# Moving the fourth group's table gathers on the Pool queue of a DLRM tower kernel, from the first group's period to a place ahead of the second group's pair products

## The reference

```python
e = jnp.stack([tbl_0[ids[:, 0]], ..., tbl_38[ids[:, 38]]], axis=1)      # 512 x 39 x 16
Xi = X0 = e
for W, b in ((W0, b0), (W1, b1), (W2, b2)):                             # 128 outputs each
    Wr = W.reshape(H, F0_, Fi)
    Xi = jnp.einsum('hjk,bjd,bkd->bhd', Wr, X0, Xi) + b[None, :, None]
    res.append(Xi.sum(axis=2))
z = jnp.concatenate(res, axis=1)
h = jnp.concatenate([z, dense_ctx], axis=1)
h = jnp.maximum(h @ W_top1 + b_top1, 0.0)
h = jnp.maximum(h @ W_top2 + b_top2, 0.0)
y = h @ W_top3
```

## Time and profile before

| | |
|---|---|
| median of 3 runs | 651.46 us (650.66 to 651.82) |
| the profiled execution's own time | 650.99 us |
| span of its trace | 649.2 us |
| PE busy | 625.8 us (96% of the span) |
| DVE busy | 563.4 us (87%) |
| ACT busy | 554.7 us (85%) |
| POOL busy | 478.2 us (74%) |
| gathers on POOL (L498) | 160, mean 954 ns |

### The profile page before, as it was taken

One profiled execution on the slowest core, in us unless ns is written; L12 is line 12 of the kernel. 1 busy time (PEld: TensorE's weight loads), 2 busy tenths in 40 slices (PEclk: granted clock), 3 DMA queues, 4 the chain that ended last, 5 costly groups with the idle time before them and its releaser, 6 DMA issues.

```text
span 649.2 us, 11457 instructions
## 1 busy us (share of the span) xinstructions
PE 625.8 (96%) x2630; PEld 478.4 (74%) x2630; DVE 563.4 (87%) x878; ACT 554.7 (85%) x1941; POOL 478.2 (74%) x533
## 2 busy tenths in 40 slices
PE   2899999999999999999999999999999999989998
PEld 2766677787777777777878777777777777767784
DVE  2658878999999999999898989999999999899880
ACT  2558889999999999999999999999999989989772
POOL 7657898888888888888888888888888647062700
PEclk9999999999999999999999999999999999999999
DMA  8264623333333242423424233333332420300000
GB/s 297 26 117 111 127 28 85 54 87 61 88 55 81 59 87 55 81 62 54 92 32 103 35 86 55 87 58 82 59 82 59 88 49 2 95 3 0 2 1 0
DMA packets 91117, 43.58 MB, mean 67 GB/s; under 512 B 80630, under 2 KB 83780, under 8 KB 88943
## 3 DMA queue, kind: packets, MB, share of 16 engines
q1 hardware_dynamic: 84058, 41.77, 29.0%
q0 software_dynamic: 5120, 1.29, 2.2%
q10 hardware_dynamic: 1904, 0.15, 0.2%
HBM read 36.39 MB, written 1.81 MB: 59 GB/s over the span
## 4 chain that ended last, share of the span: by engine, by line
PE 85%; DMA 6%; ACT 3%; POOL 2%; DVE 1%; issue 1%; SPq 1%; ACTq 0%; DVEq 0%; POOLq 0%
PE yb L1126 20%; PE yb L1130 20%; PE yb L1127 20%; PE p L1091 8%; PE pq L1103 5%; DMA late<-x_scratch 4%; DMA gram<-in_L_rec_W_dram 2%; ACT yb L767 1%; POOL late L573 1%; PE yb L1239 1%; PE p L1184 1%; PE p L1086 1%; PE p L1085 1%; PE p L1088 1%; PE p L1216 1%
## 5 line engine op out<-in xcount | busy, mean ns | idle before, releaser
L767 ACT ACTIVATE yb<-yb,x0t 128x128 f32<-128x128 f32 x1728 | 465.1, 391 | 47.7 <-PE yb L1130 44.7
L937 DVE TENSOR_TENSOR acc<-acc,yb 128x512 f32<-128x512 f32 (+1 forms) x512 | 324.3, 671 | 31.6 <-ACT yb L767 29.5
L1126 PE MATMUL yb<-w1h,x1h 128*128 128x512 f32 (+1 forms) x640 | 284.7, 445 | 4.3 <-DVE acc L937 3.3
L1130 PE MATMUL yb<-w1h,x1l 128*128 128x512 f32 (+1 forms) x640 | 247.8, 387 | 0.0
L1127 PE MATMUL yb<-w1l,x1h 128*128 128x512 f32 (+1 forms) x640 | 247.3, 386 | 0.0
L498 POOL DMA_INDIRECT emb<-in_table_dram,idx x160 | 152.6, 954 | 47.7 <-issue 44.3
L1126 PEld LDWEIGHTS yb<-w1h,x1h 128*128 128x128 f32 x640 | 120.1, 188 | 53.1 <-DVE acc L937 16.1
L1127 PEld LDWEIGHTS yb<-w1l,x1h 128*128 128x128 f32 x640 | 120.5, 188 | 34.4 <-issue 11.3
L1130 PEld LDWEIGHTS yb<-w1h,x1l 128*128 128x128 f32 x640 | 120.1, 188 | 24.9 <-DVE x1l L898 0.4
L573 POOL TENSOR_TENSOR late<-late,x0r 117x512 f32<-117x512 f32 (+1 forms) x105 | 132.7, 1295 | 5.0 <-DMA late<-x_scratch 3.9
L916 DVE TENSOR_TENSOR acc<-yb,x0t 128x512 f32<-128x512 f32 x128 | 88.1, 688 | 13.2 <-PE yb L1130 13.2
(11 more groups left out here) (125 smaller groups left out, 416.9 us busy)
## 6 DMA issues: line engine op xcount, KB each, us to landing
late<-x_scratch SPq DMA_DIRECT2D x45, 312.0 KB
late<-x_scratch SPq DMA_DIRECT2D x30, 234.0 KB
x0r<-x_scratch SPq DMA_DIRECT2D x15, 234.0 KB
emb<-in_table_dram,idx POOLq DMA_INDIRECT x160
gram<-in_L_rec_W_dram SPq DMA_DIRECT2D x1, 2496.0 KB, 11.5
late<-x_scratch SPq DMA_DIRECT2D x15, 156.0 KB
spare<-spare SPq DMA_DIRECT2D x28, 78.0 KB
x_scratch<-emb SPq DMA_DIRECT2D x75, 20.0 KB
```

Of the source, the lines that this page charges most:

```text
L767: op = act.activation(part, part, ACT.Copy, scale=x0t[u][:, t, j:j + 1])
L937: dve.tensor_tensor(part, part, parts(y_bank(t, m), n), ALU.add).then_inc(summed, 1)
L1126: pe.matmul(y[:, 0:w], hi, w1h[:, at:at + w], start=True, stop=False)
L1130: pe.matmul(y[:, 0:w], lo, w1h[:, at:at + w], start=False, stop=True).then_inc(bank_ready, 1)
```

## The change

The ten gathers of group 3 (the fourth group), with their two index additions and their two waits, leave period 0 of POOL and stand directly behind the gathers of group 2. `low_weights` moves from ahead of chunks 0 to 3 of group 1 to behind them. Period 0 of POOL holds no gathers any more; all other periods are as before.

```diff
                 if i < CHUNKS:
                     pool.wait_ge(pairs_ready, i + 1)
                 gather(0, i)
+            pool.wait_ge(embq_ready, 2)
+            pool.wait_ge(x0d_out, 16 * STORES)
+            rows_of(3, 1)
+            pool.wait_ge(idx_ready, 2 * 4)
+            for i in range(PER_Q):
+                gather(1, i)
...
             def period(g, u, after):
 
-                todo = list(range(PER_Q)) if after > 2 else []
+                ahead = isinstance(g, int) and g == 0
+                todo = list(range(PER_Q)) if after > 2 and not ahead else []
                 for t in range(TILES):
-                    if t == 0 and after > 2:
+                    if t == 0 and after > 2 and not ahead:
                         pool.wait_ge(embq_ready, g + 2)
                         pool.wait_ge(x0d_out, (g + 1) * (16 * STORES))
                         rows_of(g + 3, 1 - u)
...
-            low_weights()
             for c in range(EARLY):
                 pair_chunk(1, c)
+            low_weights()
             period(0, 0, 3)
```

## The result

| | before | changed |
|---|---|---|
| median of 18 runs of each on the same chip | 651.56 us (650.66 to 652.25) | 653.72 us (651.66 to 655.33) |
| ratio, 95% interval | | 1.0028 [1.0021, 1.0036] |
| profiled execution | 650.99 us | 651.66 us |
| its span | 649.2 us | 649.9 us |

The change makes the kernel slower by more than its measurement leaves open: 2.16 us in the medians, 0.28% in the ratio, which stands for 1.8 us. The forecast was +1.0 us, 652.5, with a top of 653.6. The median lies 0.1 us above that top; by the ratio, on the prediction's 651.46 us, the kernel comes to 653.3, inside the range near its upper end. One execution of the changed kernel took 1625.01 us and is left out of the range and the ratio; no trace shows why.

The account below looks back on a forecast made before the run. PE was taken to bound the kernel from 118 to 560 us, so earlier losses stay. New stall 2.43 us, less old 1.53, plus 0.1 remaining, gives +1.0 on 651.46: 652.5 us, 8-in-10 range 651.5 to 653.6.

Parts of the forecast that it names:

- The new stall: Chunk 0 of group 1: the ten gathers end at 56.08, so PE stands 2.43 us where it had not waited.
- The second stall and the chain: Chunk 0 of group 2: old PE stall 1.53 us; POOL and SP run later, leaving a loss of 0.90 to 1.2 us.
- the late transfer: Group 2's rows: `load_rows` and its transfer come 2.9 us later and land at 80.2 if the transfer gains nothing.
- PE's own arrival: Chunk 0 of group 2: PE gets there at 81.41 if nothing else holds it, a loss of 0.90 us.
- Cover of `bdiag`: Group 1's first tile: `bdiag` ready at 63.1, PE wants it at 63.42; covered by 0.3 us.
- The sum: First two periods: 2.43 us new stall, less 1.53 of the old, plus 0.1 remaining: +1.0 us.
- the likeliest case: Whole kernel: the forecast of +0.7 to +1.3 us, by itself 652.1 to 652.8 us; chance 0.55.
- a chain that overruns: Chunk 0 of group 2: transfer gains nothing and POOL is another 0.1 us or more late; 652.8 to 653.3; chance 0.25.
- gathers that back up: POOL ahead of group 1: gathers wait for earlier ones to land; partial back-up of 1.5 us gives 654.0; chance 0.07.
- The stall was there: Against a rival at chunk 0 of group 1: gathers fill only POOL's idle time, no new stall, 649.9; faster: 0.05.
- PE's clock falls in the longer stall: Behind the 2.43 us stall: matmuls at half speed cost 0.5 us per us; three give 654.0; chance 0.05.
- The signs that the prediction listed for being wrong: In the trace: gathers beyond 1.25 us a step, PE waiting for `bdiag`, or PE losing new time beyond 82 us.

Follow-up runs that it names:

- `e1_again`: The changed kernel run once more with no edit; 653.95 us, ratio 1.0041 to the kernel before.
- `e5_swap_alone`: The kernel before with only `low_weights` moved behind chunks 0 to 3 of group 1, gathers unmoved; 653.33 us, ratio 1.0030.
- `e6_low_first`: The changed kernel with `low_weights` put back ahead of chunks 0 to 3 of group 1, so the gathers' move alone; 655.06 us, ratio 1.0059.
- `e4_split9`: The changed kernel with nine gathers ahead and one behind `sum_dims`; 650.62 us, ratio 0.9993 to the kernel before.
- the filled kernels: The changed kernel with 20 or 10 extra identity transposes on PE ahead of chunk 0 of group 1; 0.93 and 0.83 us slower than before.
- `e2_pe_filled`: The changed kernel with 20 identity transposes on PE ahead of chunk 0 of group 1, into bank `p0`; 0.93 us slower than before.

## Where the prediction held and where it failed: its steps one by one

**The new stall: right.** The gathers ended at 55.98 (56.08 was worked out), chunk 0 on POOL began at 55.99 (56.1), and PE stood 2.38 us (2.43). PE's distance behind the product was 1.44 us, as taken from the second stall.

**The second stall and the chain: right, at the lower bound.** `load_rows` came at 66.64 (66.9), chunk 4 at 62.86 (63.1), and POOL had chunk 0 of group 2 at 79.51, where 80.34 was worked out from the late transfer. Of the two times that meet there PE's own arrival decided, with 81.37 - (79.51 + 1.44) = 0.42 us to spare. That is the lower end, +0.90; the rows give +0.86. The prediction made this hang on the transfer: from SP's issue to POOL's start it took 79.51 - 66.64 = 12.87 us, against 77.28 + 0.14 - 64.01 = 13.41 before, sooner by 0.54 us and so by more than the 0.4 that the prediction asked for. In `e1_again` it took 11.44 us, from 66.39 to 77.83, so it also differs from one execution to the next.

**Cover of `bdiag`: held.** PE's matmul on it runs at 63.38 without a wait.

**The sum: right for what it counted.** +1.0 was taken. The kernel that keeps PE working through the same lateness is slower by 0.93 us, and the profiled execution by 0.7. What was measured beyond that the sum didn't hold, and the likeliest case, 652.1 to 652.8 us, missed it. That 653.3 by the ratio still lies in the range is luck: the range was drawn up to 653.6 for a chain that overruns and gathers that back up, and neither happened. In the prediction's terms the kernel came out slower, with an interval that starts at 0.21%; "slower" had 0.37, "same" 0.58.

**The rivals that fell.** The chain didn't overrun. The gathers didn't back up: each of the ten came 0.30 us behind the one ahead of it. The stall was there.

**The step that failed: the rival "PE's clock falls in the longer stall" got 0.05.** It was weighed by the stop of 1.53 us, in which the earlier trace rows and behind which (81 to 83 us, below) the granted clock stayed at 1.00; from that it was concluded for a stop of 2.4 us, which no row showed. The runs show that a stop of this length is one behind which the fall can occur: 2.05 us in `e1_again`, 2.74 in `e5_swap_alone`, 3.56 in `e6_low_first`. Its price was sized nearly right, though the three us at half speed stood on no row: 1.5 us were worked out, the two executions of the changed kernel give 1.60. Added to the stall's own 0.93 us it makes 2.5 us; the medians of the two comparisons of the changed kernel are 2.16 and 2.90 us above before. The signs that the prediction listed for being wrong were gathers, `bdiag` and time lost beyond 82 us; none looked at the matmuls right behind the new stall, where the loss lay. The Trainium skill ("TensorE: Matmul & The Clock Gate", Part 1) says that an idle array's clock is halved. In `e1_again` the granted clock behind the stop is indeed 0.50.

The trace before holds what may be a sign that was passed over. Its column of the granted clock shows 1.00 everywhere, also at 14 to 16 us, behind PE's first 10.85 us without work:

```profile
14.00:16.00 2.00, 2.00 (x11) 2.00 (x11) 0.40 (x1) 0.85 (x2) 1.67 (x2) 1.00 1.03 369
...
24.00:26.00 2.00, 2.00 (x19) 1.86 (x18) 2.00 (x5) 0.00 (x0) 1.39 (x3) 1.00 0.30 44
...
81.00:83.00 2.00, 2.00 (x9) 1.42 (x8) 1.47 (x3) 0.63 (x2) 2.00 (x3) 1.00 0.23 31
```

But PE gets through only 11 small matmuls there, as many as in `e4_split9` at a clock of 0.50, against 19 at 24 to 26 us. Most likely it ran at half clock at the start, and the pace of the matmuls shows what the column doesn't; no run settles this.

How often it falls can be read only from the times, not execution by execution. Of the 22 times of the changed kernel 6 lie between 651.66 and 652.74 us, about where the filled kernels lie (651.21 to 652.34), and 16 lie between 653.07 and 655.33. So some three in four carry something of the fall's size.

**What stays open.** Why the clock falls behind a stop in one execution and not in the next isn't settled: 2.38 us without a fall, 2.05 us with one (2.21 and 1.88 us of idle time in the rows). The preparation of the weights gives more cases, at PE's wait for DVE ahead of sixteen matmuls (22.34 in the first profile of the changed kernel). Waits of 0.81 us (before), 1.83 (`e2_pe_filled`), 1.92 (`e5_swap_alone`) and 1.96 (`e1_again`) were followed by no fall; in the five other executions the waits were 2.52 to 3.29 us, and each was followed by one. Taken together the two places overlap, so the runs don't give a length at which it begins. Times up to 655.33 us are more than the stall and a fall of 1.60 us make, and no trace shows them; a longer fall (2.44 us in `e6_low_first`) or one more in the preparation (`e4_split9`) could do it, which isn't shown.

## What to carry to other kernels

Count a queue's idle time before filling it: POOL had room for some six gathers ahead of the pair products, six of them gained 1.49 us, ten cost 2.2. A stop of the matrix engine that is made longer can cost more than its length, because the work behind it may run at half clock: here one of 1.53 us cost its own length, one of about 2.4 us by the times some 1.6 us more in most executions, and a sum over stalls needs a line for it whenever a stop becomes longer than any that the trace shows at full clock. Where such a stop can't be avoided, a few matmuls that nobody reads, in a bank that is overwritten anyway, can keep the clock; here they saved 1.97 us.

## What the runs showed of the hardware that was not expected

What a fall of the clock costs depends on whether PE is what the others wait for. In the first profiled execution of the changed kernel it fell at 22 to 24 us, behind a wait of 2.97 us:

```profile
22.34 3.42 PE L1035 MATMUL yb<-ident,w2t 128*128 128x128 f32 x16 [2.97 <-DVE w1l L900]
```

Sixteen small matmuls took 3.42 us, 2.45 before, yet at 54.82 PE was where it had been at 54.88 before. The longer fall at the same place in `e4_split9`, from about 20 to 28 us, was not free: POOL's gathers started 1.3 us later there, PE's last matmul ahead of the stop 1.6 us later, and the execution took 1.31 us more than the median of its kernel. Therefore a mean granted clock of 0.997 doesn't tell an execution's time. Of the kernel before, 23 executions in the two batches have a mean clock of 1.000 and a median of 651.0 us, 25 have 0.997 and 651.15 us (one has 0.995, 652.30 us). The changed kernel has 0.997 in the profiled 651.66 us, where the fall is in the weights' preparation, and 0.997 in the 653.07 us of `e1_again`, where it is behind the stall. One has to look at the stretch in which the clock falls.
